# VectorE's order inside the attention of a gated cross-attention and mixture-of-experts block: low halves of the queries ahead of the residual and the means, first-chunk statistics at other places

## The chip, the cores and the metric

The kernel runs on one core of a Trainium2 chip. The metric is the device time of one execution in microseconds; a profiled execution also has a span, from its first to its last instruction. The core's engines are TensorE (PE, with its weight loads as PEld), VectorE (DVE), ScalarE (ACT), GpSimd (POOL) and SyncE (SP), which issues all DMAs here. Each runs its own list of instructions in order and waits on semaphores.

## The reference

```
x: 32 batches x 128 tokens x 128;  ctx: 32 x 128 x 64;  16 heads of 64
q = layernorm(x) @ Wq;  k = ctx @ Wk;  v = ctx @ Wv
x = x + tanh(g_xattn) * (softmax(q k^T / 8) v @ Wo + bo)
h = layernorm(x)
s = sigmoid(h @ gate_w^T); 2 of 4 groups, then 8 of 32 experts, weights s / sum(s) * 2.5
x = x + tanh(g_ffn) * (sum of the taken experts' silu(h Wg) * (h Wu) Wd + one shared expert)
```

All of it is float32. The kernel splits an operand of a product into a high part, rounded to the fast format, and a low part, the rest, and adds three products (high by high, low by high, high by low).

## The kernel before

The 32 batches go in 8 chunks of 4 batches (`CB = 4`). The first 385 us or so are the attention, one batch t after the other; the rest are the experts, chunk by chunk. Each engine has its own function `attention(c, first, last)`, which `in_chunks` calls for the first chunk, then in a hardware loop for the six middle ones, then for the last. What is in a function is the engine's order, written out by hand. A batch has two halves of its heads (h = 0, 1), so VectorE counts eight steps in a chunk: `step_of_chunk = 2 * b + h`.

TensorE, in batch t: `max_scores` (L1146) makes scores of batch t+2, of which VectorE's `take_max` (L762) takes the row maxima; `scores` (L1166 to L1175) makes the exact scores of batch t; `transpose_max` (L1156) turns the maxima of batch t+1; `weigh` (L1186) multiplies by the context; `project_out` (L1210) projects batch t-3. In the odd batches (b = 1 and 3) `g_project` (L1110 to L1112) makes the projected queries for two later batches, in four banks of PSUM. Banks 0 and 1 are the same that `max_scores` writes. ScalarE copies each bank to the high halves (`g_high`, L514) and VectorE subtracts to make the low halves (`g_low`, L753). TensorE waits for these twice:

```
pe.wait_ge(glo_ready, 4 * nth + 2)          # max_scores, b even and h == 0: banks 0 and 1 are free
pe.wait_ge(glo_ready, 4 * (...) + 4)        # scores, h == 0: all four low halves are there
```

and before `g_project` may write banks 0 and 1, it waits for `take_max` of h = 1.

VectorE normalises the weighed sums of batch t-2 (`normalise`, L776, one for each half of the partitions q = 0, 1). For this the reciprocals of the sums (`invert`, L770) go to DRAM and come back spread over partitions (`inverse_bc`), two DMAs in a row on SyncE's queue. VectorE then adds the projection to x (`residual`, L786) for batch t-3. `transpose_max` of the next batch waits for that residual, since both use the bank `small_ps`. From chunk 1 on VectorE also takes the statistics of the second layer norm: `batch_stats`, `batch_mean` (L685) and, once in a chunk in its last batch, `keep_means` (L690).

The first layer norm's statistics (`chunk_stats`, L671 and L674) are taken chunk by chunk during chunk 0: `STATS_AT` says in which step. `LN_AT` says in which steps the twelve levels of the reciprocal root of chunk 1 (`rstd_level`) go; `ln_apply(1)` follows them, and with it TensorE's `transpose_norm` (L1117). In step 7 all levels for chunks 2 to 7 are done at once. The last chunk starts with the second layer norm: after `take_max` and `batch_stats` VectorE does `rstd_level` for 24 batches and `ln2_apply`, and TensorE's `transpose_norm` waits for it.

Of the kernel before, what the change touches and what calls it, by code (L numbers as in the profile page):

```python
# [32 lines left out]
NB = 32  # L33
# [3 lines left out]
CB = 4  # L37
# [17 lines left out]
RSTD_LEVELS = 3 + 3 * NEWTON_STEPS  # L55
# [9 lines left out]
WBC_GROUPS = (UNITS - 1) // 2  # L65
WEIGHTS_AT = 14
X2_AT = 15
LN_AT = {0: range(0, 5), 1: range(5, 9), 2: range(9, RSTD_LEVELS)}
AHEAD = 2
STATS_AT = {3: (2,), 4: (3,), 5: (4,), 6: (5, 6), 7: (7,)}  # L70
NB_SEAM = (NCH - 2) * CB
SEAM = {4: (1, 7), 5: (7, 13), 6: (13, 16), 7: (16, 21)}
LATE = {NB - 2: 5, NB - 1: 11}
# [3 lines left out]
def build(nc, x, ctx_nat, ctx_t, g_xattn, g_ffn, wq_t, wk_t, wv_t, wo, bo, router_t, router_bias, experts, out):  # L77
    with ExitStack() as stack:  # L78
# [6 lines left out]
        def raw(ap):  # L85

            return ap.bitcast(F32)
# [571 lines left out]
        def _(dve):  # L659
# [8 lines left out]
            def chunk_stats(n):  # L668

                for b in range(CB):  # L670
                    nc.vector.bn_stats(bn6[:, 0, b, :], tile_of(CB * n + b)).then_inc(ln_step[0], 1)  # L671
                wait_first(ln_step[0], 2 * CB * n + CB)
                for b in range(CB):
                    nc.vector.bn_aggr(mean_var[:, 0, CB * n + b, :], bn6[:, 0, b, :]).then_inc(ln_step[0], 1)  # L674
                dve.wait_ge(ln_step[0], 2 * CB * (n + 1))

            def batch_stats(t, b):

                wait_first(x2_ready, t + 1)
                nc.vector.bn_stats(bn6[:, 1, b, :], tile_of(t)).then_inc(ln_step[1], 1)  # L680
# [11 lines left out]
            def rstd_level(which, n, batches, level):  # L692

                width = batches.stop - batches.start
                scratch = ln_small if width <= 2 * CB else ln_large
                v, w, bits, first_guess, odd_guess, even_guess, square, product = (
                    scratch[:, k, 0:width] for k in range(8))
                variance, base, stepped = mean_var[:, which, batches, 1], RSTD_STEPS * n, rstd_step[which]
                i, newton_op = divmod(level - 3, 3)
                if level == 0:  # L700
                    if which:
                        dve.wait_ge(means_kept, batches.stop // CB)
                    else:
                        dve.wait_ge(ln_step[0], 2 * batches.stop)
                    nc.vector.tensor_scalar(v, variance, EPS, None, ALU.add).then_inc(stepped, 1)
                    nc.vector.tensor_scalar(w, variance, EPS, -0.5, ALU.add, ALU.mult).then_inc(stepped, 1)
                elif level == 1:

                    dve.wait_ge(stepped, base + 2)
                    nc.vector.tensor_scalar(bits.bitcast(I32), v.bitcast(I32), 1, 0x7fffffff,  # L710
                                            ALU.logical_shift_right, ALU.bitwise_xor).then_inc(stepped, 1)
                elif level == 2:
                    dve.wait_ge(stepped, base + 3)
                    nc.vector.tensor_scalar(first_guess, bits, GUESS_SCALE, None, ALU.mult).then_inc(stepped, 1)
                else:

                    guesses = (first_guess, odd_guess, even_guess, rstd[:, which, batches])
                    dve.wait_ge(stepped, base + level + 1)
                    if newton_op == 0:
                        ins = nc.vector.tensor_tensor(square, guesses[i], guesses[i], ALU.mult)  # L720
                    elif newton_op == 1:
                        ins = nc.vector.tensor_tensor(product, square, w, ALU.mult)
                    else:
                        ins = nc.vector.scalar_tensor_tensor(guesses[i + 1], product, 1.5, guesses[i], ALU.add, ALU.mult)
                    ins.then_inc(stepped, 1)
# [8 lines left out]
            def ln_apply(n, t):  # L734

                dve.wait_ge(rstd_step[0], RSTD_STEPS * (n + 1 if isinstance(n, int) and n < AHEAD else AHEAD + 1))
                wait(dve, xt_done, n)
                apply(0, t)
# [11 lines left out]
            def g_low(g, ring, banks=range(4)):  # L750
                for j in banks:
                    dve.wait_ge(ghi_ready, 4 * g + j + 1)
                    nc.vector.tensor_tensor(g_lo[:, ring, 2 * j:2 * j + 2, :],  # L753
                                            bank[j][:].rearrange("p (h n) -> p h n", h=2),
                                            raw(g_hi[:, ring, 2 * j:2 * j + 2, :]), ALU.subtract)\
                        .then_inc(glo_ready, 1)
# [15 lines left out]
            def normalise(t, parity, q):  # L772

                dve.wait_ge(inverse_in, 32 * t + 32)
                wait(dve, attn_done, t - 1)
                nc.vector.tensor_tensor(u_t[rows(q), parity, :, :].rearrange("p i n -> p (i n)"),  # L776
                                        u_raw[parity][rows(q), q, :, :].rearrange("p h n -> p (h n)"),
                                        inverse_bc[rows(q), :, :].rearrange("p h n -> p (h n)"), ALU.mult)\
                    .then_inc(norm_ready[q], 1)
# [175 lines left out]
            dve.wait_ge(router_in, 32)  # L955
            dve.wait_ge(x_in[1], 16)
            dve.wait_ge(const_ready, 6)

            def attention(c, first, last):
                for b in range(CB):  # L960
                    t = CB * c + b
                    for h in range(2):
                        step_of_chunk = 2 * b + h
                        if not (last and b >= 2):
                            for q in range(2):
                                take_max(t + 2, b % 2, h, q)

                        if h == 0:
                            if not first:
                                batch_stats(t - CB, b)  # L970
                        else:
                            if not (first and b == 0):
                                invert(t - 1, (b - 1) % 2)
                            if not (first and b < 2):
                                normalise(t - 2, b % 2, 1)
                            if not (first and b < 3):
                                residual(t - 3)
                            if not first:
                                batch_mean(t - CB, b)
                                if b == CB - 1:  # L980
                                    keep_means(t - b - CB)
                        if first:
                            if step_of_chunk == 0:
                                chunk_stats(1)
                            for level in LN_AT.get(step_of_chunk, ()):
                                rstd_level(0, 1, slice(CB, 2 * CB), level)
                            if step_of_chunk == 2:
                                ln_apply(1, CB)
                        elif not last and step_of_chunk == 1:
                            ln_apply(c + 1, t - b + CB)  # L990
                        if last:
                            if step_of_chunk == 0:
                                for level in range(RSTD_LEVELS):
                                    rstd_level(1, 0, slice(0, NB_SEAM), level)
                                ln2_apply(0, 0)
                            if step_of_chunk == 4:
                                ln2_apply(1, CB)
                            if step_of_chunk in SEAM:
                                route_chunk_0(*SEAM[step_of_chunk])
                        if h == 0 and not (first and b < 2):  # L1000
                            normalise(t - 2, b % 2, 0)
                        if h == 1 and b % 2 == 1 and not last:
                            g_low(2 * c + 2 + b // 2, b // 2)
                        if step_of_chunk == 2 and not last:
                            xt_low(c + 1)
                        if step_of_chunk == 3 and last:
                            route_levels[0](0, ut_ps)
                        if first:
                            for n in STATS_AT.get(step_of_chunk, ()):
                                chunk_stats(n)  # L1010
                            if step_of_chunk == 7:
                                for level in range(RSTD_LEVELS):
                                    rstd_level(0, 2, slice(2 * CB, NB), level)

            in_chunks(dve, attention)
            residual(NB - 3)
# [388 lines left out]
```

## Time and profile before

| | |
|---|---|
| median of 3 runs | 693.19 us (692.09 to 695.07) |
| profiled execution, its own time | 695.34 us |
| its span | 693.5 us |
| mean granted TensorE clock | 0.989 |
| PE busy | 662.6 us (96% of the span) |
| DVE busy | 504.2 us (73%) |
| ACT busy | 369.2 us (53%) |
| POOL busy | 285.8 us (41%) |

Busy time of a pipelined matmul is modelled, so a busy PE may still wait a little inside it. The profiled execution took 2.15 us longer than the median.

### The profile page before, as it was taken

The page shows a single profiled execution, that of the slowest core. Times are in us where ns is not written, and L with a number is a line of the kernel's source. Part 1 is how long each engine was busy: PE and PEld are TensorE (multiplying, and loading weights), DVE is VectorE, ACT ScalarE, POOL GpSimd, SP SyncE. Part 2 cuts the span into 40 slices and gives each one's busy share as a digit, 9 for nine tenths or more (in the row PEclk, how much of TensorE's full clock was granted, in tenths as well). Part 3 has the DMA queues.
Part 4 walks back from the last instruction along what each step waited for, and adds up shares of the span by engine and source line. Part 5 has one row for each costly group of instructions (what it writes and reads, how often), then busy time and mean ns, then how long its engine had stood idle before and what let it go on. Part 6 is the DMA issues. An engine that isn't in the chain of part 4 may idle for free. (4 is left out here: it accounts for less than half of the span.)

```text
span 693.5 us, 13643 instructions
## 1 busy us (share of the span) xinstructions
PE 662.6 (96%) x3676; PEld 477.5 (69%) x3676; DVE 504.2 (73%) x1329; ACT 369.2 (53%) x691; POOL 285.8 (41%) x317
## 2 busy tenths in 40 slices
PE   8998999999999999999899899999999999999997
PEld 6555666666556666666556778878787888888785
DVE  5877876766757577685866886969687786869565
ACT  4363454554545555555465445555555555565553
POOL 4213131332323222232320555656565665756564
PEclk9998999999999999999999999999999999999999
DMA  7322222323223222332223825555353636464550
GB/s 192 80 61 72 58 71 64 89 60 76 59 76 80 69 77 60 76 88 62 54 58 94 186 62 127 135 113 138 81 136 86 160 80 153 107 149 114 124 139 15
DMA packets 63244, 65.58 MB, mean 95 GB/s; under 512 B 26080, under 2 KB 41568, under 8 KB 63200
## 3 DMA queue, kind: packets, MB, share of 16 engines
q1 hardware_dynamic: 63200, 65.07, 38.5%
q8 instruction: 18, 0.29, 0.2%
q14 instruction: 26, 0.21, 0.1%
HBM read 61.64 MB, written 2.88 MB: 93 GB/s over the span
## 5 line engine op out<-in xcount | busy, mean ns | idle before, releaser
L494 POOL TENSOR_TENSOR halves<-area,halves 128x512 fp32r<-128x512 f32 x135 | 175.2, 1298 | 147.8 <-ACT halves L620 142.7
L633 ACT ACTIVATE area<-bank 128x512 f32<-128x512 f32 x136 | 81.4, 599 | 113.8 <-PE bank L1112 112.9
L574 ACT ACTIVATE area<-bank 128x512 f32<-128x512 f32 x128 | 69.5, 594 | 129.8 <-PE bank L1175 129.8
L1068 DVE TENSOR_TENSOR bank<-area,bank 128x512 f32<-128x512 f32 x128 | 88.7, 693 | 54.9 <-PE bank L1112 54.6
L1186 PE MATMUL bank<-area,ctx_keys 128*65 128x512 f32 (+1 forms) x256 | 127.4, 611 | 0.8 <-ACT u_odd L528 0.8
L1110 PE MATMUL bank<-x2t_hi,w_hi 128*128 128x512 f32 x272 | 110.8, 407 | 1.6 <-DVE area L1078 1.6
L762 DVE TENSOR_REDUCE row_max<-bank 128x4 f32<-128x512 f32 x128 | 81.9, 682 | 35.0 <-PE bank L1146 32.5
L440 POOL TENSOR_TENSOR ctx_hi<-ctx_raw,ones_col 128x128 fp32r<-128x128 f32 x32 | 18.0, 562 | 216.4 <-DMA ctx_raw<-ctx_t 216.4
L1111 PE MATMUL bank<-x2t_hi,w_lo 128*128 128x512 f32 x272 | 107.1, 394 | 0.0
L1112 PE MATMUL bank<-x2t_lo,w_hi 128*128 128x512 f32 x272 | 106.4, 391 | 0.0
L620 ACT ACTIVATE halves<-area 128x512 fp32r<-128x512 f32 x136 | 85.0, 626 | 18.9 <-DVE area L1078 18.6
L1078 DVE TENSOR_TENSOR area<-bank,wbc 128x512 f32<-128x512 f32 x128 | 86.5, 681 | 0.4 <-DMA wbc<-rows_dram 0.4
L776 DVE TENSOR_TENSOR area<-u_odd,inverse_bc 64x1024 f32<-64x1024 f32 x32 | 41.1, 1283 | 45.1 <-DMA inverse_bc<-inverse_dram 44.6
L1210 PEld LDWEIGHTS bank<-c_pair,area 128*128 128x128 f32 x512 | 62.8, 196 | 14.4 <-issue 11.7
L1210 PE MATMUL bank<-c_pair,area 128*128 128x128 f32 x512 | 64.1, 280 | 3.1 <-DVE area L776 2.0
L1186 PEld LDWEIGHTS bank<-area,ctx_keys 128*65 128x65 f32 (+1 forms) x256 | 38.0, 166 | 41.8 <-issue 40.2
L1110 PEld LDWEIGHTS bank<-x2t_hi,w_hi 128*128 128x128 f32 x272 | 51.3, 189 | 14.7 <-DVE area L1078 4.5
L1112 PEld LDWEIGHTS bank<-x2t_lo,w_hi 128*128 128x128 f32 x272 | 51.2, 188 | 12.1
L1146 PEld LDWEIGHTS bank<-ctx_hi,halves 64*128 64x128 f32 x512 | 33.5, 186 | 36.7 <-issue 29.8
L1111 PEld LDWEIGHTS bank<-x2t_hi,w_lo 128*128 128x128 f32 x272 | 51.4, 189 | 10.2
L1110 PE MATMUL bank<-halves,w_hi 128*128 128x512 f32 x136 | 54.3, 399 | 1.1 <-POOL halves L494 1.1
L1112 PE MATMUL bank<-halves,w_hi 128*128 128x512 f32 x136 | 53.9, 396 | 0.0
(129 smaller groups left out, 1106.5 us busy)
## 6 DMA issues: line engine op xcount, KB each, us to landing
wbc<-rows_dram SPq DMA_DIRECT2D x128, 256.0 KB, 4.3
inverse_bc<-inverse_dram SPq DMA_DIRECT2D x64, 256.0 KB, 3.9
w_raw<-experts SPq DMA_DIRECT2D x32, 102.0 KB, 2.0
ctx_raw<-ctx_t SPq DMA_DIRECT2D x32, 64.0 KB, 1.9
ctx_keys<-ctx_nat SPq DMA_DIRECT2D x32, 64.0 KB, 2.1
out<-area SPq DMA_DIRECT2D x7, 256.0 KB, 4.0
max_rows<-max_t SPq DMA_DIRECT2D x64, 4.0 KB
area<-wq_t SPq DMA_DIRECT2D x1, 512.0 KB, 4.5
```

Source lines behind the costliest of these rows:

```text
L494: nc.gpsimd.tensor_tensor(hid_lo[:, u % SLOTS, :], hid[:, u % HIDS, :], raw(hid_hi[:, u % SLOTS, :]), ALU.subtract).then_inc(hidlo_ready, 1)
L574: nc.scalar.activation(probs_t[:, k, :, :], st_ps[q][:].rearrange("p (h n) -> p h n", h=4), ACT.Exp)\
L620: nc.scalar.activation(hid_hi[:, u % SLOTS, :], hid[:, u % HIDS, :], ACT.Copy).then_inc(hidhi_ready, 1)
L633: nc.scalar.activation(silu_g[:, u % 2, :], gate_ps[u % 2][:], ACT.Silu).then_inc(silu_ready, 1)
L762: nc.vector.tensor_reduce(row_max[:, parity, first:first + 4], ps[q][:].rearrange("p (h m) -> p h m", h=4), AX_X, ALU.max)\
L1068: nc.vector.tensor_tensor(up_ps[u % UPS][:], silu_g[:, u % 2, :], up_ps[u % UPS][:], ALU.mult)\
L1078: nc.vector.tensor_tensor(hid[:, u % HIDS, :], up_ps[u % UPS][:], wbc[:, group % WBC_SLOTS, i, :], ALU.mult).then_inc(hid_ready, 1)
L1110: nc.tensor.matmul(ps, wh, xh, start=start, stop=False)
L1111: nc.tensor.matmul(ps, wl, xh, start=False, stop=False)
L1112: return nc.tensor.matmul(ps, wh, xl, start=False, stop=stop)
L1186: nc.tensor.matmul(u_ps[q][0:CD + 1 if q == 0 else P, :], keys, probs_t[:, k, :, :].rearrange("p i n -> p (i n)"), start=True, stop=True). ...
L1210: ins = nc.tensor.matmul(ps, u_t[:, parity, p, :], c_pair[:, p, :], start=p == 0, stop=p == PAIRS - 1)
```

## The change

Nothing is computed differently and no instruction is added or removed: VectorE's instructions in the attention stand in another order. (1) In the odd batches `g_low` goes right behind `normalise(t - 2, 1)`, ahead of `residual`, `batch_mean` and `keep_means`. (2) `chunk_stats(1)` goes ahead of the loop. (3) The levels for chunk 1 are done in steps 0 and 1, and `ln_apply(1)` in step 2 has none left ahead of it. (4) `chunk_stats(2)` to `(7)` go to steps 2, 3, 4, 5 and 6 (two of them), and inside their step ahead of `g_low`, `residual` and `normalise(t - 2, 0)`, where before they stood at the end.

```diff
-LN_AT = {0: range(0, 5), 1: range(5, 9), 2: range(9, RSTD_LEVELS)}
+LN_AT = {0: range(0, 8), 1: range(8, RSTD_LEVELS)}
-STATS_AT = {3: (2,), 4: (3,), 5: (4,), 6: (5, 6), 7: (7,)}
+STATS_AT = {2: (2,), 3: (3,), 4: (4,), 5: (5,), 6: (6, 7)}
             dve.wait_ge(const_ready, 6)
+            chunk_stats(1)
...
-                        if h == 0:
-                            if not first:
-                                batch_stats(t - CB, b)
-                        else:
+                        if h == 0 and not first:
+                            batch_stats(t - CB, b)
+                        if h == 1:
                             if not (first and b == 0):
                                 invert(t - 1, (b - 1) % 2)
                             if not (first and b < 2):
                                 normalise(t - 2, b % 2, 1)
+                        if step_of_chunk == 2 and first:
+                            ln_apply(1, CB)
+                        if first:
+                            for n in STATS_AT.get(step_of_chunk, ()):
+                                chunk_stats(n)
+                        if h == 1 and b % 2 == 1 and not last:
+                            g_low(2 * c + 2 + b // 2, b // 2)
+                        if h == 1:
                             if not (first and b < 3):
                                 residual(t - 3)
                             if not first:
...
                         if first:
-                            if step_of_chunk == 0:
-                                chunk_stats(1)
                             for level in LN_AT.get(step_of_chunk, ()):
                                 rstd_level(0, 1, slice(CB, 2 * CB), level)
-                            if step_of_chunk == 2:
-                                ln_apply(1, CB)
...
-                        if h == 1 and b % 2 == 1 and not last:
-                            g_low(2 * c + 2 + b // 2, b // 2)
...
-                        if first:
-                            for n in STATS_AT.get(step_of_chunk, ()):
-                                chunk_stats(n)
-                            if step_of_chunk == 7:
-                                for level in range(RSTD_LEVELS):
-                                    rstd_level(0, 2, slice(2 * CB, NB), level)
+                        if first and step_of_chunk == 7:
+                            for level in range(RSTD_LEVELS):
+                                rstd_level(0, 2, slice(2 * CB, NB), level)
```

## Rows read from the trace of the kernel before

**Rows 1.** The page: busy time, share of the span and instructions of each engine.

```profile
PE 662.6 (96%) x3676; PEld 477.5 (69%) x3676; DVE 504.2 (73%) x1329; ACT 369.2 (53%) x691; POOL 285.8 (41%) x317
```

**Rows 2.** TensorE's waits in the attention, 0 to 390 us: total, times, longest.

```profile
PE bank L1146 <- DVE halves L753: 3.6, 5, 0.9
...
PE bank L1166 <- DVE halves L753: 3.0, 11, 0.3
```

**Rows 3.** Timeline of VectorE, last batch of chunk 1: start, duration, idle before.

```profile
97.75 1.29 DVE L762 TENSOR_REDUCE row_max<-bank 128x4 f32<-128x512 f32 x2 [2.11 <-PE bank L1146]
...
106.77 1.22 DVE L776 TENSOR_TENSOR area<-u_odd,inverse_bc 64x1024 f32<-64x1024 f32 x1 [4.10 <-DMA inverse_bc<-inverse_dram]
...
110.69 0.29 DVE L786 TENSOR_TENSOR x_sb<-bank,x_sb 128x128 f32 x1
...
111.32 0.54 DVE L690 COPY mean_var<-mean_var_now 128x8 f32 x1 [0.25 <-DVE mean_var_now L685]
111.78 2.47 DVE L753 TENSOR_TENSOR halves<-bank,halves 128x512 fp32r<-128x512 f32 x4
```

**Rows 4.** Timeline of TensorE at the same place, into chunk 2.

```profile
113.46 0.66 PE L1146 MATMUL bank<-ctx_hi,halves 64*128 64x128 f32 x8 [0.85 <-DVE halves L753]
114.38 0.50 PE L1166 MATMUL bank<-halves,ctx_hi 64*128 64x512 f32 x2 [0.26 <-DVE halves L753]
...
115.51 0.28 PE L1156 MATMUL bank<-ident,row_max 128*16 128x128 f32 x1
```

**Rows 5.** Timeline of ScalarE at the same place: the four high halves.

```profile
109.73 2.65 ACT L514 ACTIVATE halves<-bank 128x512 fp32r<-128x512 f32 x4 [0.66 <-PE bank L1112]
```

**Rows 6.** Timeline of VectorE, second batch of chunk 1.

```profile
89.42 0.29 DVE L786 TENSOR_TENSOR x_sb<-bank,x_sb 128x128 f32 x1
...
89.71 2.45 DVE L753 TENSOR_TENSOR halves<-bank,halves 128x512 fp32r<-128x512 f32 x4
```

**Rows 7.** Timeline of TensorE, the same batch.

```profile
92.22 0.50 PE L1166 MATMUL bank<-halves,ctx_hi 64*128 64x512 f32 x2 [0.23 <-DVE halves L753]
```

**Rows 8.** Timeline of VectorE and TensorE from chunk 6 to chunk 7.

```profile
330.81 2.47 DVE L753 TENSOR_TENSOR halves<-bank,halves 128x512 fp32r<-128x512 f32 x4
...
338.42 0.66 PE L1117 MATMUL bank<-ident,xn 128*128 128x128 f32 x4 [1.92 <-DVE xn L730]
```

**Rows 9.** Timeline of VectorE in chunk 0.

```profile
27.33 1.29 DVE L762 TENSOR_REDUCE row_max<-bank 128x4 f32<-128x512 f32 x2 [2.09 <-PE bank L1156]
...
48.34 1.22 DVE L776 TENSOR_TENSOR area<-area,inverse_bc 64x1024 f32<-64x1024 f32 x1 [1.86 <-DMA inverse_bc<-inverse_dram]
...
50.89 1.29 DVE L762 TENSOR_REDUCE row_max<-bank 128x4 f32<-128x512 f32 x2
...
59.26 1.22 DVE L776 TENSOR_TENSOR area<-u_odd,inverse_bc 64x1024 f32<-64x1024 f32 x1 [2.90 <-DMA inverse_bc<-inverse_dram]
60.40 0.85 DVE L671 BATCH_NORM_STATS2 bn<-x_sb 128x6 f32<-128x128 f32 x4
...
63.25 1.29 DVE L762 TENSOR_REDUCE row_max<-bank 128x4 f32<-128x512 f32 x2
```

**Rows 10.** Timeline of TensorE in chunk 0 and at the start of chunk 1.

```profile
32.77 0.66 PE L1146 MATMUL bank<-ctx_hi,halves 64*128 64x128 f32 x8 [0.55 <-issue]
...
52.28 0.66 PE L1146 MATMUL bank<-ctx_hi,halves 64*128 64x128 f32 x8 [1.79 <-issue]
...
64.04 0.55 PE L1110 MATMUL bank<-xnt_hi,a_hi 128*128 128x256 f32 x1 [2.22 <-issue]
...
75.38 0.66 PE L1146 MATMUL bank<-ctx_hi,halves 64*128 64x128 f32 x8 [0.51 <-DVE row_max L762]
```

**Rows 11.** Windows: length, busy PE, PEld, DVE, ACT, POOL, granted clock, DMA.

```profile
52.00:58.00 6.00, 5.72 (x28) 3.20 (x29) 4.12 (x13) 2.82 (x6) 2.81 (x4) 0.72 0.37 91
64.00:68.00 4.00, 3.96 (x22) 3.99 (x23) 3.30 (x6) 1.39 (x3) 0.81 (x2) 0.61 0.07 20
203.00:208.00 5.00, 5.00 (x20) 2.51 (x16) 1.63 (x3) 2.41 (x5) 0.00 (x0) 0.66 0.01 2
```

## The prediction

> **What bounds the kernel now.** I read the page first: TensorE is busy 96% of the span [rows 1], so the time is its work plus the few places where it stands. The change touches only VectorE's order in the attention, so I took TensorE's waits there next and looked for those that end on something VectorE does later than it must. Two groups of them end on the low halves: before `max_scores`, 3.6 us in 5 waits, and before `scores`, 3.0 us in 11 waits [rows 2]. Then I laid the timelines of the two engines side by side, at a chunk's end, in the second batch of a chunk, and through chunk 0, where the largest single waits stand: 1.79 and 2.22 us [rows 10]. Idle time of VectorE itself says nothing here, but where it idles shows what its later work is tied to.
>
> **Part 1, low halves first: chunks 1 to 6.** At the end of a chunk VectorE is free at 110.69, does the residual, the mean and the kept means, and begins the low halves at 111.78 [rows 3]. Put first, they begin 111.78 - 110.69 = 1.09 us earlier. Two other things could hold them. ScalarE ends the fourth high half at 109.73 + 2.65 = 112.38 [rows 5]; the fourth low half is a quarter of 2.47, 0.62 us, and moved forward it would start at 110.69 + 3 x 0.62 = 112.55: later than that, so ScalarE just doesn't bind. And TensorE without its two waits would begin `scores` 0.85 + 0.26 = 1.11 us earlier [rows 4]. The three agree: about 1.1 us at this boundary. At the other boundaries the two waits are smaller, and the sum of all is what counts.
>
> In the second batch the low halves move by 89.71 - 89.42 = 0.29 us [rows 6] and TensorE waits 0.23 for them [rows 7]; so 0.23 to 0.29, six times.
>
> The waits view gives all of it at once: 3.6 + 3.0 = 6.6 us are waits for the low halves [rows 2]. Five of the boundaries and six second batches make the 5 and the 11. I take 6.4, a little less, since ScalarE binds at some of them. None of it needs VectorE to be faster: it has the same work, and what is moved behind (residual, mean, kept means, 1.09 us together) is done while TensorE runs `max_scores` and `scores`. The next thing that TensorE needs from VectorE there comes much later.
>
> Does an earlier TensorE stay earlier? In the following half chunk VectorE waits twice for TensorE or for a DMA: at 97.75 `take_max` waited 2.11 for TensorE, and at 106.77 `normalise` waited 4.10 for the spread reciprocals [rows 3]. That DMA chain begins with the `take_max` that TensorE released, so it moves with TensorE, and the shift is carried to the next boundary.
>
> At the sixth boundary, from chunk 6 to chunk 7, it is not carried. There the low halves begin at 330.81, and VectorE then works without a pause up to the normalised tokens for which TensorE waits 1.92 us at 338.42 [rows 8]. The order of VectorE's work in this stretch changes, its amount doesn't; TensorE will do its part about 0.9 earlier and wait about 2.8 instead of 1.9. This boundary gives nothing, and isn't in the 6.4.
>
> **Part 2, statistics of chunk 0.** `chunk_stats(1)` stood behind the `take_max` of 27.33 and ahead of the next. That first one had waited 2.09 us for TensorE [rows 9]; ahead of the loop the statistics run in this wait, and fit: half of the pair's 2.85 us (60.40 to 63.25) is 1.43. TensorE's wait of 0.55 at 32.77 [rows 10] goes. I count 0.55, and 0.3 more for the earlier `ln_apply(1)`, since the levels 9 to 11 are no longer between. `chunk_stats(3)` now stands ahead of the first low halves of the chunk: -0.3.
>
> Then come two places of one kind. At 48.34 `normalise` starts, when its DMA has landed, and `take_max` follows only at 50.89; of these 2.55 us, 1.14 are `normalise` (as from 59.26 to 60.40) and 1.41 a `chunk_stats` [rows 9]. TensorE stood 1.79 us, until 52.28, for that `take_max` [rows 10]. With the statistics ahead of `normalise`, inside the 1.86 us that it waited for the DMA, 1.41 go out of the chain. The DMA and TensorE are both about 0.6 earlier by then (0.55 + 0.3 - 0.3), so the wait falls to 1.79 - 1.41 = 0.4: 1.4 gained. The second place has two `chunk_stats`, from 60.40 to 63.25, 2.85 us, between the `normalise` of 59.26, which waited 2.90 for its DMA, and the `take_max` of 63.25 that releases `g_project` at 64.04, after 2.22 us of standing [rows 9, 10]. Now they go into the 2.90 us: a near fit. The DMA itself starts with the reciprocals behind the first place, 0.6 + 1.4 = 2.0 earlier; TensorE comes 0.6 + 1.4 + 1.6 = 3.6 earlier, the last term the clock's, below. So it will stand 2.22 + 3.6 - 2.0 - 2.85 = 1.0: 1.2 to 1.3 gained on the wait. Last, `chunk_stats(7)` no longer follows the low halves, so the wait of 0.51 at 75.38 [rows 10] goes: 0.4 to 0.5, of which 0.3 is already in the start of `scores`. Sum of the waits: 0.55 + 0.3 - 0.3 + 1.4 + 1.3 + 0.35 = 3.6 us.
>
> **The clock.** After each of the two long waits TensorE was granted its lower clock: 0.72 of the full clock in 6.00 us and 0.61 in 4.00 us [rows 11]. The levels are 2.4 and 1.2 GHz. The loss is 6.00 x 0.28 = 1.7 and 4.00 x 0.39 = 1.6, of which a part fell on time when TensorE stood anyway; I take 3.0 for both. With waits of 0.4 and 1.0 in place of 1.79 and 2.22 they are about as short as those at the five boundaries (3.6 in 5, the longest 0.9 [rows 2]), of which one was followed by a low clock (203 to 208, 0.66, 5.00 x 0.34 = 1.7 [rows 11]). So I expect both losses gone; the bounds are 0 and 3.3. The one at 203 may go too (1.7), as its wait does, and a new one may come after the wait of 2.8 ahead of chunk 7, priced like the others at 1.5: these two I set against each other.
>
> The Trainium skill (TensorE: Matmul & The Clock Gate, section "The HAM clock gate") says that the array's clock is gated to one of two levels by how busy the array has been; its section "HAM oscillation" names idle gaps as what brings it down. By that the longer gap ahead of chunk 7 speaks against this change. The trace so far is undecided on it: a wait of 1.92 us there left the clock at full, while 1.79 and 2.22 in chunk 0 did not.
>
> **Sum.** 6.4 + 3.6 + 3.0 = 13.0 us. Against the profiled execution's own time, 695.34, that is 682.3; a lost low clock at 203 would take 1.7 more, 680.6. The median of the runs is 2.15 us below the profiled one, about one such loss. From the median: 693.19 - 13.0 = 680.2 us.
>
> **The rivals.**
> - *The clock falls anyway.* The waits go, but in chunk 0 or ahead of chunk 7 the clock still falls once or twice. For it: both remaining waits in chunk 0 aren't zero, the one ahead of chunk 7 grows. Against it: four of five boundary waits left it alone. It gives back 1.5 to 4.5: 683.2 (682 to 685).
> - *The round trip of the reciprocals binds instead.* If the DMAs' landing doesn't move with TensorE, what is gained before `scores` is lost before `g_project`, whose `take_max` comes right behind the `normalise` that waited 4.10 [rows 3]. The 6.4 go, the rest stays: 693.19 - 6.6 = 686.6. If chunk 0 is also tied to it, 3 to 4 more are lost, about 690 or no change at all. Against it: the chain starts at a `take_max` that waited for TensorE [rows 3].
> - *The late residual costs more than it gave* (the other side). `transpose_max` of the next batch waits for the residual, which now stands behind the low halves. By rows it ends at 110.69 + 2.47 + 0.29 = 113.45, and `transpose_max`, at 115.51 before [rows 4], would be due at 114.4: 0.95 us to spare. Each us beyond that is paid by TensorE in 12 places. To end over 0.5% slower it must eat 13.0 + 3.5 = 16.5, so be 1.4 us beyond the spare in each: about 697. Nothing in the rows makes the low halves that late.
>
> **Chances and range.** The forecast (waits and low clocks both gone, 680.2, own range 678 to 682.5) 0.60; the clock falls anyway 0.17; the round trip binds in the loop (686.6) 0.10; it binds in chunk 0 too or the gain vanishes otherwise (690 to 696) 0.08; slower 0.05. The low end takes in the extra loss at 203: 680.2 - 1.7, and 1.5 for chunk 0's waits going altogether, 677. The high end reaches to 687, which holds the first rival and the second's value: 0.85 or so inside. 0.5% of 693.19 is 3.5 us, about what a measurement of this kernel can tell from no change; faster by more than that 0.89, within it 0.07, slower 0.04.
>
> **What would show it.** In the profile after: the waits of L1146 and L1166 on the low halves nearly gone from TensorE's list (under 1 us together); the low halves right behind `normalise` in both odd batches; TensorE's waits in chunk 0 near 0.4 (`max_scores`) and 1.0 (`g_project`); granted clock 1.00 from 50 to 70 us; a wait near 2.8 ahead of the last chunk's first `transpose_norm`; `transpose_max` without a wait for the residual; the loop's chunks 1.0 to 1.3 us shorter each. I am wrong if the DMA wait before `normalise` grows in the loop by as much as `scores` starts earlier, if a VectorE wait shows up before `transpose_max`, or if the clock is low as often as before.

## The result and the profile after

The changed kernel takes 682.81 us (median of 4 runs, 680.67 to 683.44), the kernel before 693.62 in the same comparison: a ratio of 0.9839 (95% interval 0.9808 to 0.9870). By that ratio it is 11.2 us less (9.0 to 13.3); the two medians are 10.8 apart. Run a second time, beside another kernel, it came to 0.9831 (0.9803 to 0.9860). The forecast was 680.2, in a range of 677 to 687. The time is inside the range and faster by more than 0.5%, but 0.3 above the forecast's own range of 678 to 682.5, where the first rival (the clock falls anyway, 682 to 685) stood.

The profiled execution took 683.27 us (span 681.5, mean granted clock 0.995). The page's first row beside [rows 1]: the work of each engine is the same within 3 us, while the span is 12.0 shorter.

```profile
PE 659.6 (97%) x3676; PEld 476.5 (70%) x3676; DVE 501.3 (74%) x1329; ACT 368.5 (54%) x691; POOL 286.8 (42%) x317
```

TensorE's waits from 0 to 390 us (total, times, longest), against [rows 2]. In the changed kernel the lines of the file are one less from `g_project` on: L1145 is `max_scores`, L1165 `scores`, L1109 `g_project`, L1116 `transpose_norm`, L1155 `transpose_max`. `<- issue` means that the profile shows nothing for which the engine waited.

```profile
PE bank L1116 <- DVE xn L730: 2.8, 1, 2.8
...
PE bank L1109 <- DVE row_max L762: 1.8, 4, 0.7
...
PE bank L1109 <- issue: 0.9, 1, 0.9
PE bank L1145 <- issue: 0.8, 1, 0.8
PE bank L1165 <- DVE halves L753: 0.7, 3, 0.3
```

The 3.6 us of `max_scores` for the low halves are gone altogether, and of the 3.0 of `scores` 0.7 are left. Nothing of the same size has come in their place but the first row, the wait for the normalised tokens ahead of the last chunk, which grew from 1.92 [rows 8] to 2.81.

The end of chunk 1 on VectorE, against [rows 3], and on TensorE, against [rows 4]:

```profile
101.22 1.22 DVE L776 TENSOR_TENSOR area<-u_odd,inverse_bc 64x1024 f32<-64x1024 f32 x1 [3.99 <-DMA inverse_bc<-inverse_dram]
...
105.30 2.48 DVE L753 TENSOR_TENSOR halves<-bank,halves 128x512 fp32r<-128x512 f32 x4
107.70 0.28 DVE L786 TENSOR_TENSOR x_sb<-bank,x_sb 128x128 f32 x1
...
108.99 1.29 DVE L762 TENSOR_REDUCE row_max<-bank 128x4 f32<-128x512 f32 x2 [0.50 <-issue]
```

```profile
107.00 0.66 PE L1145 MATMUL bank<-ctx_hi,halves 64*128 64x128 f32 x8
107.92 0.50 PE L1165 MATMUL bank<-halves,ctx_hi 64*128 64x512 f32 x2 [0.26 <-DVE halves L753]
...
109.05 0.28 PE L1155 MATMUL bank<-ident,row_max 128*16 128x128 f32 x1
```

Read from the landing of the reciprocals, the start of `normalise`: the low halves begin 105.30 - 101.22 = 4.08 us after it, before it was 111.78 - 106.77 = 5.01; `scores` begins 6.70 after it, before 7.61. So 0.9 here, where the sum had 1.1; the second `normalise`, between the two, ran 1.45 us in this execution, before 1.29. The DMA wait ahead of the first `normalise` is 3.99, before 4.10: the landing has moved along with TensorE. `residual` now ends at 107.98, and `transpose_max` starts at 109.05 without waiting for it, 1.1 us later.

Over five chunks, from the low halves at 111.78 to those at 330.81 [rows 3, 8] there were 219.0 us. In the changed kernel:

```profile
316.14 2.48 DVE L753 TENSOR_TENSOR halves<-bank,halves 128x512 fp32r<-128x512 f32 x4
```

that is 210.8 us from 105.30 to 316.14, 8.2 less. 1.7 of them are the low clock at 203 [rows 11], which is absent; 6.5 are the order, where 6.4 had been counted for the loop (with one second batch more). So close a match is partly luck. The kernel before, with its low clock taken off, is at 217.3 us for this stretch; `busy_chunk0` and `stats_only` below, which have the old order there, took 216.3 and 215.7, and seven further profiles with the new order 209.5 to 212.2. The means of old and new are 5.8 apart.

Chunk 0 on VectorE, against [rows 9], and on TensorE, against [rows 10]:

```profile
47.26 1.22 DVE L776 TENSOR_TENSOR area<-area,inverse_bc 64x1024 f32<-64x1024 f32 x1 [0.60 <-DMA inverse_bc<-inverse_dram]
48.40 1.27 DVE L762 TENSOR_REDUCE row_max<-bank 128x4 f32<-128x512 f32 x2
51.36 0.25 DVE L770 RECIPROCAL inverse<-sums 128x16 f32<-128x16 f32 x1 [1.69 <-DMA sums<-u_odd]
...
58.38 1.22 DVE L776 TENSOR_TENSOR area<-u_odd,inverse_bc 64x1024 f32<-64x1024 f32 x1
59.53 1.27 DVE L762 TENSOR_REDUCE row_max<-bank 128x4 f32<-128x512 f32 x2
```

```profile
50.73 0.66 PE L1145 MATMUL bank<-ctx_hi,halves 64*128 64x128 f32 x8
...
60.30 0.36 PE L1109 MATMUL bank<-xnt_hi,a_hi 128*128 128x256 f32 x1 [0.91 <-issue]
...
69.71 0.66 PE L1145 MATMUL bank<-ctx_hi,halves 64*128 64x128 f32 x8
```

At both places `take_max` now follows `normalise` at once. TensorE doesn't stand before `max_scores` any more (1.79 before) and 0.91 before `g_project` (2.22 before). The last row answers to the one of 75.38: 5.7 us earlier, and this execution had entered chunk 0 about 0.7 later than the one before, by the `max_scores` that stands ahead of all that the change moves (22.37 against 21.70). So chunk 0 gave 6.3; 6.6 had been counted. The entry lies anywhere from 21.3 to 22.6 in the profiles here, whatever the kernel, so times in chunk 0 are compared from the entry on. From there to the first `max_scores` of chunk 1 are 53.7 us in the kernel before, 47.3 here and 47.2 in its second profile (`changed_again`).

The windows (length, busy PE, PEld, DVE, ACT, POOL, granted clock, DMA), against [rows 11]:

```profile
50.00:56.00 6.00, 5.73 (x34) 2.90 (x33) 4.40 (x15) 3.23 (x8) 3.41 (x5) 1.00 0.33 89
60.00:66.00 6.00, 5.65 (x42) 4.35 (x42) 5.76 (x16) 3.29 (x6) 3.34 (x5) 1.00 0.16 36
320.00:328.00 8.00, 5.19 (x22) 3.83 (x21) 5.30 (x21) 2.82 (x6) 1.55 (x3) 0.79 0.12 26
```

The clock is at its upper level, 2.4 GHz, through chunk 0, but it is low behind the wait of 2.81 us ahead of the last chunk: 8.00 x 0.21 = 1.7 us. 6.3 + 6.5 - 1.7 = 11.1. The runs show 11.2 and, the second time, 11.7. (A further low stretch, at the end of the attention, is in both of these profiles and cancels; it comes up again in the last section.)

### The profile page after: what moved, and what is told of

The parts are those of the page before. It is cut to its first block and busy times, and to the rows that moved or that the text cites. A ratio compares the mean times of both kernels' runs of the same rounds, so it can differ in the third digit from the quotient of the medians.

```text
span 681.5 us, 13645 instructions
## 1 busy us (share of the span) xinstructions
PE 659.6 (97%) x3676; PEld 476.5 (70%) x3676; DVE 501.3 (74%) x1329; ACT 368.5 (54%) x691; POOL 286.8 (42%) x317
## 5 line engine op out<-in xcount | busy, mean ns | idle before, releaser
L1185 PE MATMUL bank<-area,ctx_keys 128*65 128x512 f32 (+1 forms) x256 | 125.0, 600 | 1.2 <-ACT u_odd L528 1.0
L1109 PE MATMUL bank<-x2t_hi,w_hi 128*128 128x512 f32 x272 | 110.5, 406 | 1.6 <-DVE area L1077 1.6
L1109 PEld LDWEIGHTS bank<-x2t_hi,w_hi 128*128 128x128 f32 x272 | 51.2, 188 | 14.8 <-DVE area L1077 4.5
L1109 PE MATMUL bank<-halves,w_hi 128*128 128x512 f32 x136 | 54.3, 399 | 1.1 <-POOL halves L494 1.1
L1145 PEld LDWEIGHTS bank<-ctx_hi,halves 64*128 64x128 f32 x512 | 33.4, 186 | 29.0 <-issue 23.0
```

What stands on the lines that cost most here:

```text
L1109: nc.tensor.matmul(ps, wh, xh, start=start, stop=False)
L1185: nc.tensor.matmul(u_ps[q][0:CD + 1 if q == 0 else P, :], keys, probs_t[:, k, :, :].rearrange("p i n -> p (i n)"), start=True, stop=True). ...
```

## The experiments

All ratios are to the kernel before, run in the same comparison.

**Each part alone.** `low_first` is the kernel before with the low halves moved and nothing else:

```diff
                             if not (first and b < 2):
                                 normalise(t - 2, b % 2, 1)
+                            if b % 2 == 1 and not last:
+                                g_low(2 * c + 2 + b // 2, b // 2)
...
-                        if h == 1 and b % 2 == 1 and not last:
-                            g_low(2 * c + 2 + b // 2, b // 2)
```

> Only part 1 of the change: the low halves ahead of residual, mean and kept means in the odd batches; the statistics of chunk 0 as before. My theory: TensorE's waits for the low halves (3.6 and 3.0 us before) all but vanish, the loop gives 6.4 us, the wait ahead of chunk 7 grows from 1.9 to 2.8 us and may cost 1.7 by a low clock, and chunk 0 with its two low clocks stays as before: 5 to 6.5 us under the kernel before, ratio 0.991 to 0.993. Rival (the round trip of the reciprocals binds): the waits move to before g_project and the time is that of before, ratio 1.000.

Measured: 687.37 us, 0.9917 (0.9890 to 0.9943), which is 5.8 us less. Its wait ahead of the last chunk is 2.82, with a low clock behind it (0.66 from 330 to 335).

`stats_only` is the changed kernel with `g_low` back at its old place:

```diff
-                        if h == 1 and b % 2 == 1 and not last:
-                            g_low(2 * c + 2 + b // 2, b // 2)
...
                         if h == 0 and not (first and b < 2):
                             normalise(t - 2, b % 2, 0)
+                        if h == 1 and b % 2 == 1 and not last:
+                            g_low(2 * c + 2 + b // 2, b // 2)
```

> Only part 2: the statistics and levels of chunk 0 at their new places, the low halves behind residual and means as before. My theory: chunk 0 is 6 us shorter (3.3 of it waits, 3.0 the clock, which stays full), nothing changes in the loop: ratio 0.990 to 0.992. With low_first the two parts add up to the whole change (0.984). Rival (chunk 0's gain is given back to the DMAs later): ratio 0.996 or more.

Measured: 686.80 us, 0.9919 (0.9888 to 0.9950). TensorE's waits for the low halves are back in full:

```profile
PE bank L1145 <- DVE halves L753: 3.6, 5, 0.9
PE bank L1165 <- DVE halves L753: 3.3, 12, 0.3
```

The parts give 0.83% and 0.81%, together 1.64%; the whole change gives 1.61% and, the second time, 1.69%. They add up, and each is worth half.

**The last batch alone.** `low_first_b3` moves the low halves only where the kept means stood before them:

```diff
+                            if b == 3 and not last:
+                                g_low(2 * c + 2 + b // 2, b // 2)
...
-                        if h == 1 and b % 2 == 1 and not last:
+                        if h == 1 and b == 1 and not last:
                             g_low(2 * c + 2 + b // 2, b // 2)
```

> Part 1 only in the last batch of each chunk; the second batch's low halves stay behind residual and mean. My theory: 4.9 of the loop's 6.4 us come from here and 1.5 from the second batches, so 5 us less than before minus up to 1.7 by a low clock ahead of the last chunk: 688.5 to 690, ratio 0.993 to 0.996. Rival (it is the second batches that count, or both are needed): 0.998 or more.

Measured: 688.32 us, 0.9952 (0.9935 to 0.9970), 3.3 us less, as expected with the low clock taken off; the profile shows that low clock (0.66 from 330 to 335). The waits of `scores` (L1168 in this run) for the low halves that remain are 1.5 us in 7 times, which is the share of the second batches.

**The clock ahead of the last chunk.** `busy_seam` gives TensorE something to do in the wait:

```diff
+                    if last and b == 0:
+                        keep_busy(3, ut_ps)
                     if b == (0 if last else 1):
                         transpose_norm(c + 1, ut_ps)
```

> The changed kernel, and TensorE runs three idle products into a free bank ahead of the last chunk's first transpose_norm, where it stood 2.8 us. My theory: the granted clock, which fell to 0.72 in the 5 us behind that wait, stays at full there, and the time is 1.7 us under the changed kernel's: ratio to before 0.981 to 0.982, median about 681. Rival (the clock has nothing to do with that wait, or the products push the transposes back): 0.984 or more, 683 us.

Measured: 681.07 us, 0.9831 (0.9807 to 0.9856). The wait is 0.25 us and the clock full, in the window in which it was 0.79 before:

```profile
320.00:328.00 8.00, 7.75 (x46) 4.69 (x44) 5.72 (x16) 2.37 (x5) 1.57 (x3) 1.00 0.12 26
```

That the clock was full in the profiled execution is shown. A gain in the time is not: the changed kernel, run again (below), has the same ratio, 0.9831. The 1.7 us between the medians 682.81 and 681.07 are from different comparisons, in which the kernel before also differed, by 0.4.

`seam_first` makes the wait itself shorter, by order again:

```diff
+                        if last and step_of_chunk == 0:
+                            for level in range(RSTD_LEVELS):
+                                rstd_level(1, 0, slice(0, NB_SEAM), level)
+                            ln2_apply(0, 0)
                         if not (last and b >= 2):
                             for q in range(2):
                                 take_max(t + 2, b % 2, h, q)
...
                         if last:
-                            if step_of_chunk == 0:
-                                for level in range(RSTD_LEVELS):
-                                    rstd_level(1, 0, slice(0, NB_SEAM), level)
-                                ln2_apply(0, 0)
```

> The changed kernel with another order at the start of the last chunk: the reciprocal roots of 24 batches and ln2_apply ahead of take_max and batch_stats. My theory: the normalised tokens are ready 1.4 us earlier (two row maxima of 1.2 and statistics of 0.2), TensorE waits 1.4 instead of 2.8 us for them, the clock stays at full (1.7), and max_scores of h = 1, due 3 us later, doesn't yet miss the maxima: 3 us under the changed kernel, ratio to before 0.979 to 0.981. Rival: the late maxima hold max_scores of h = 1, so only the place of the wait changes: 0.984.

Measured: 679.74 us, 0.9805 (0.9780 to 0.9831). Since that was close to the changed kernel's interval, both were run once more side by side.

> The changed kernel itself once more, beside seam_again on the same chip, so that the two can be compared. Ratio to before as first measured, 0.984; the wait ahead of the last chunk is 2.8 us again, and the clock behind it may be low or full in the one profile.

> The kernel seam_first once more beside the changed kernel. My theory: the wait ahead of the last chunk is 1.1 to 1.4 us shorter and the clock behind it full, 1 to 3 us under the changed kernel, ratio to before 0.980 to 0.982. Rival: what the first run showed was another chip's spread, and the two are within 1 us.

Measured: 680.84 us for the changed kernel and 679.08 for the other, 0.9831 (0.9803 to 0.9860) and 0.9811 (0.9783 to 0.9839). TensorE at the same place, first the changed kernel, then `seam_first` in its second run:

```profile
324.36 1.12 PE L1116 MATMUL bank<-ident,xn 128*128 128x128 f32 x4 [2.81 <-DVE xn L730]
```

```profile
322.32 0.66 PE L1116 MATMUL bank<-ident,xn 128*128 128x128 f32 x4 [1.37 <-DVE xn L730]
```

The duration of the transposes, 1.12 against 0.66, is the clock. The wait is 1.4 shorter (1.1 in the first run), and the gain 1.8 us where 3 were expected: the direction came out twice, the size is within the scatter of the runs. Beside `busy_seam`, in one comparison with it, `seam_first` is 1.3 us faster, about what its wait is shorter; so by the medians it is the shorter wait that pays, though these intervals overlap too. It is the fastest of the kernels here by both comparisons, though its interval overlaps that of the changed kernel.

**How much room the residual has.** The rival on the other side was that the residual behind the low halves holds `transpose_max`. Extra work between the two measures it; it computes nothing.

```diff
                         if h == 1 and b % 2 == 1 and not last:
                             g_low(2 * c + 2 + b // 2, b // 2)
+                            for _ in range(1):
+                                nc.vector.memset(x2t[:], 0.0)
```

> The changed kernel with one VectorE memset of 128x512 (0.48 us by the row of another such) between the low halves and the residual, in the 14 odd batches that have low halves. It delays the residual, and with it transpose_max. My theory: there are 0.9 us to spare before transpose_max, so nothing happens, 683 us, ratio to before 0.984 to 0.986 (at the start of the last chunk it adds its 0.5). Rival (the residual is already the bound): each of 14 batches pays 0.5, 690 us, 0.994.

Measured: 681.47 us, 0.9853 (0.9815 to 0.9892); TensorE has no wait before `transpose_max`. The memset took 0.48 us and made the residual 0.5 late. `residual_4` has in its place

```diff
+                            nc.vector.memset(raw(x2t_hi[:]), 0.0)
+                            nc.vector.memset(raw(x2t_lo[:]), 0.0)
```

> The same with two memsets of 128x1024, some 1.9 us together. My theory: 0.9 us are to spare, so transpose_max comes 1.0 late in 14 batches, TensorE waits for it directly, and 1.9 more are lost ahead of the last chunk: 682.8 + 14 + 1.9 = 698, ratio 1.005 to 1.008. Rival (later cover, nothing but the last chunk's start pays): 685, 0.988.

Measured: 695.79 us, 1.0055 (1.0035 to 1.0075). TensorE's waits in its attention (L1157 is `transpose_max`, L1118 `transpose_norm`):

```profile
PE bank L1157 <- issue: 8.0, 7, 1.2
PE bank L1157 <- DVE x_sb L786: 6.1, 6, 1.0
PE bank L1118 <- DVE xn L730: 3.7, 1, 3.7
```

Thirteen waits of about 1.1 us, 14.1 in all. Each memset took 0.91 us, and with what lies between them the residual came at 110.20 instead of about 108.1, 2.1 us later at the boundary after chunk 1. So the room is 2.1 - 1.0 = 1.0 to 1.1 us (0.95 had been worked out); beyond it every microsecond is TensorE's. The price of that rival was right (1.1 us in 13 places, where 12 were counted), its condition was not met.

**Maxima ahead of the reciprocals.** `max_first` is `seam_first` with this in the odd batches:

```diff
-                        if h == 0 and not (first and b < 2):
+                        if h == 0 and not (first and b < 2) and (last or b % 2 == 0):
                             normalise(t - 2, b % 2, 0)
...
                             if not (first and b < 2):
+                                if not last and b % 2 == 1:
+                                    normalise(t - 2, b % 2, 0)
                                 normalise(t - 2, b % 2, 1)
```

> The kernel with the better start of the last chunk (seam_first), and in the odd batches of the first seven chunks normalise of q = 0 comes behind take_max and invert of h = 1 instead of ahead of them: the maxima that release g_project no longer stand behind the landing of the reciprocals. My theory: TensorE's short waits before g_project (0.2 to 0.7 us, 1.7 in chunk 0) go, but the second normalise and the low halves still stand behind the same landing, 1.2 us more of work between it and them minus 1.4 of maxima and invert, so what is won before g_project is mostly given back before scores: 677 to 680 us, ratio 0.977 to 0.981. Rival (low halves later than now): 683 or more.

Measured: 678.79 us, 0.9800 (0.9769 to 0.9831), no different from `seam_first`. The waits before `g_project` for the maxima left the list. Those before `scores` for the low halves returned, and in chunk 0 `max_scores` stood 1.4 us for them, with a low clock behind it (0.72 from 64 to 70):

```profile
PE bank L1167 <- DVE halves L753: 3.1, 12, 0.3
```

**The head of chunk 0.** `head_back` is the changed kernel with `chunk_stats(1)` and the levels of chunk 1 at their old places:

```diff
-LN_AT = {0: range(0, 8), 1: range(8, RSTD_LEVELS)}
+LN_AT = {0: range(0, 5), 1: range(5, 9), 2: range(9, RSTD_LEVELS)}
...
-            chunk_stats(1)
...
+                            if step_of_chunk == 0:
+                                chunk_stats(1)
```

> The changed kernel, but chunk_stats(1) and the levels of chunk 1 stand where they stood before; the other statistics keep their new places. My theory in the prediction gave the head 0.85 us. By the profile after, the later chain of reciprocals took up what was won there, so 0.3 or less is lost: 683 us, ratio 0.984 to 0.985. Rival (the head is worth its 0.85 or more): 683.7 or more.

Measured: 681.90 us, 0.9851 (0.9822 to 0.9880). That is 10.3 us under the kernel before, where the changed kernel has 11.2 and 11.7; the intervals overlap. In the profile the wait of 0.54 before `max_scores` is back, and TensorE starts `g_project` at 60.59, the changed kernel at 60.30. That looks like 0.3 us, but this execution entered chunk 0 at 21.30, 1.1 earlier:

```profile
21.30 1.11 PE L1148 MATMUL bank<-ctx_hi,halves 64*128 64x128 f32 x16 [0.35 <-ACT max_t L521]
...
69.98 0.66 PE L1148 MATMUL bank<-ctx_hi,halves 64*128 64x128 f32 x8
```

From the entry on, chunk 0 takes 48.7 us here, against 47.3 and 47.2 in the two profiles of the changed kernel. So the head is worth about 1.3 us in the profiles and 0.9 to 1.4 by the ratios. That is at least the 0.85 of the prediction, and not the "0.3 or less" expected before the run.

**The first low clock of chunk 0.** `busy_chunk0` is the kernel before with

```diff
+                    if first and b == 3:
+                        keep_busy(2, ut_ps)
```

ahead of the `max_scores` that stood 1.79 us.

> The kernel before, and TensorE runs two idle products (1.8 us) into a free bank where it stood 1.79 us for the maxima in the fourth batch of chunk 0. The question is whether the low clock behind that wait cost anything. The prediction counted 1.6 us for it. Theory from the run low_first, whose chunk 0 has the same order and had a full clock there: the next step, g_project, stands for the reciprocals' round trip, which starts at VectorE's take_max and not at TensorE's arrival, so with a full clock TensorE only stands longer before it (3.4 to 3.6 instead of 2.2 us), and the time is that of before, ratio 0.998 to 1.001. Rival (the prediction's term): 1.6 us less, ratio 0.9975.

Measured: 692.81 us, 1.0018 (0.9996 to 1.0040). The clock is full where it was 0.72, and TensorE stands longer at the next place:

```profile
50.00:56.00 6.00, 6.00 (x29) 2.82 (x29) 5.58 (x19) 2.90 (x7) 3.34 (x5) 1.00 0.23 60
62.00:68.00 6.00, 4.41 (x24) 4.45 (x25) 4.96 (x13) 1.68 (x3) 1.75 (x4) 0.72 0.13 42
```

```profile
50.68 1.88 PE L1225 MATMUL bank<-c_pair 128*128 128x512 f32 x4
...
63.59 0.54 PE L1110 MATMUL bank<-xnt_hi,a_hi 128*128 128x256 f32 x1 [3.19 <-issue]
```

`g_project` starts at 63.59 against 64.04 [rows 10], after 3.19 us of standing against 2.22, and the clock behind that is low as before. Both executions entered chunk 0 at 21.7, and the first `max_scores` of chunk 1 comes at 75.09, before at 75.38. A clock that is full only up to the next wait earned 0.3 us at most in the profile, and nothing in the times.

## Why the prediction was right, and where its sizes were off

**The low halves.** Right in mechanism and size: 6.4 counted; 6.5 in the profiled five chunks, 5.8 in the mean of all profiles, and 5.8 us by `low_first`, which isolates it. The waits view had both the places and the sum. That the shift is carried to the next boundary was right too; the DMA wait before `normalise` stayed at 4.0. The second rival, the round trip that doesn't move with TensorE, is out for the loop.

**The seam to the last chunk.** That the sixth boundary gives nothing, and the wait there becomes 2.8, came out to 0.01 us (2.81 in both profiles of the changed kernel, and 2.80 to 2.82 in three more kernels). The step that failed is the one after it: "these two I set against each other", a possible gain at 203 against a possible loss here. The gain at 203 can't be taken from the median, only from the one profiled execution that had the loss; the loss at the seam came in both profiles of the changed kernel and in most others. Without that offset the sum from the median is 680.2 + 1.7 = 681.9. The two ratios, put on the 693.19 of the prediction, give 682.0 and 681.5. That lies about midway between the forecast and the first rival's 683.2, so the time alone doesn't tell them apart. But the rival's condition, a low clock ahead of chunk 7, was met in both profiles, and 0.17 was too little for it.

**Chunk 0.** The sum of 6.6 was nearly right (6.3), and most of its steps come out when times are taken from the entry of chunk 0:
- The head gave what was counted. The `max_scores` at 43.3 us, in both profiles, is 0.65 earlier when counted from the entry, where 0.55 to 0.85 were due, and putting the head back cost 1.3 in the profile (`head_back`).
- The shift of the reciprocals that start the second round trip, 2.0, came out in `changed_again`: 50.47, which is 28.4 after its entry (22.05), against 52.10 and 30.4 before. In the first profile it was only 1.4, since there the reciprocals waited 1.69 us for the DMA that brings the sums. `changed_again`, `stats_only`, `seam_first` and `residual_1` don't have this wait.

```profile
50.47 0.25 DVE L770 RECIPROCAL inverse<-sums 128x16 f32<-128x16 f32 x1
...
57.95 1.22 DVE L776 TENSOR_TENSOR area<-u_odd,inverse_bc 64x1024 f32<-64x1024 f32 x1 [0.49 <-DMA inverse_bc<-inverse_dram]
```

- The start of `g_project` moved by 4.4 us in the first profile and 4.5 in the second, where 2.0 + 2.85 = 4.85 were due by the prediction's own account of VectorE. The first low clock, 1.6 of the 3.0 for the clock, hardly enters there: the prediction adds it to TensorE's gain and takes it off again in the longer wait. Taken alone it was worth nothing (`busy_chunk0`). In chunk 0 VectorE and the reciprocals' round trip set the pace, and what TensorE loses between two of its waits only shortens the next wait. So the term that was off is this one. It was a gain only as far as TensorE, at the low clock, would have come too late for the earlier `g_project`: 4.85 - (2.0 + 2.22) = 0.6 us by the prediction's numbers, not 1.6.
- The second low clock did cost its 1.4. From the start of `g_project` to the next `max_scores` TensorE works through, 64.04 to 69.27 before, 60.30 to 64.17 after: 5.23 us against 3.87. It isn't taken up behind: `g_project` to the first `max_scores` of chunk 1 is 1.9 us shorter, and 1.36 of that and the 0.51 us wait there make it up.

```profile
69.27 0.66 PE L1146 MATMUL bank<-ctx_hi,halves 64*128 64x128 f32 x8
```

```profile
64.17 0.66 PE L1145 MATMUL bank<-ctx_hi,halves 64*128 64x128 f32 x8
```

The statistics taken out from between `normalise` and `take_max`, 1.41 and 2.85, count in full, because VectorE is the path here: `take_max` went from 63.25 to 59.53, 3.7 earlier and 4.4 with the later start.

**The late residual.** Not met, and now measured: the room is about 1 us, and an overdraft is paid 13 times.

## What to carry to other kernels

When an engine that is always busy stands for another engine's result, list what that other engine does between being free and beginning that result; if one of those pieces of work is needed only after the result would be finished, do the result first. Then measure the room that is left with a dummy instruction, since whatever goes beyond it is paid in every round. Work put behind a wait that is there anyway is free only as long as it fits, and it must stand ahead of the waiting instruction, not behind it. Time won on one engine, its clock included, counts only up to its next wait on a chain that doesn't start with it: find that wait before adding terms. And before the times of two profiles are compared in a stretch, take out the offset with which each entered it.

## What the runs showed of the hardware

The granted clock behind a wait of TensorE isn't a matter of its length alone. At the seam, waits of 2.80 to 2.82 us were followed by a low clock in four profiles (the changed kernel twice, `low_first`, `low_first_b3`) and by a full one in `head_back`:

```profile
320.00:325.00 5.00, 2.20 (x16) 1.54 (x15) 4.15 (x16) 1.63 (x3) 0.00 (x0) 1.00 0.16 33
325.00:330.00 5.00, 5.00 (x39) 3.14 (x39) 3.08 (x7) 2.20 (x4) 1.57 (x3) 1.00 0.06 9
```

A wait of 3.30 us there had a low clock behind it (`residual_1`), one of 3.69 a full one (`residual_4`). Waits of 1.37 to 1.92 us left it full in the kernel before, `stats_only`, `busy_chunk0`, `max_first` and both runs of `seam_first`, while in chunk 0 of the kernel before 1.79 us was followed by a low clock [rows 10, 11], and so was one of 0.93 us at 201 us of that profile.

At the end of the attention every kernel here has a wait of 1.88 to 1.99 us, for `normalise`. Behind it the clock is low in seven of the fourteen profiles (the kernel before, the changed kernel twice, `stats_only`, `head_back`, `residual_4`, the second of `seam_first`) and full in the other seven. The changed kernel and the first `seam_first` at this place:

```profile
375.00:380.00 5.00, 4.45 (x21) 4.30 (x22) 4.34 (x9) 1.46 (x4) 1.27 (x1) 0.66 0.44 97
```

```profile
373.00:378.00 5.00, 4.87 (x29) 4.34 (x30) 4.94 (x11) 2.66 (x6) 1.78 (x2) 1.00 0.44 109
```

Each low stretch is 1.4 to 1.7 us of TensorE's work by its window, so single profiled executions of one kernel can differ by that much. The Trainium skill (TensorE: Matmul & The Clock Gate, section "The HAM clock gate") has the clock go down for how busy the array has been; the runs agree in so far as filling the wait with products went with a full clock at both places where that was tried, in one profile each, though the clock was full without it too at both places in other profiles (`head_back` behind 2.80 us ahead of the last chunk, `low_first_b3` behind 1.37 us in chunk 0).
